# Splitting expert tails in place, another order on VectorE, and first-slot rows from one-hot products on TensorE

## The reference, cut to what matters

```
c = x @ W.T + ((x @ A[a].T) @ B[a].T) * scaling[a]     # a = adapter of the batch row
li = round(c @ w_gate.T * 128); shifted = clip(li - max(li), -128)
two largest shifted per token, ties to the lower expert; weights from an exp table, made to sum to 1
out = sum over experts e of weight_e * ((silu(c @ w1[e].T) * (c @ w3[e].T)) @ w2[e].T)
result = x + out                                        # hidden width 704 = 5 * 128 + 64
```

## Time and profile before

| | us |
|---|---|
| median of 3 runs (lowest, highest) | 231.97 (231.13, 232.19) |
| the profiled execution's own time | 231.47 |
| its span, from first to last instruction | 229.4 |
| PE busy | 205.3 |
| POOL busy | 150.7 |
| DVE busy | 100.7 |
| ACT busy | 85.5 |

### The profile page before, as it was taken

How to read it: one execution, slowest core, us unless ns; L and a number is a source line. 1 busy time by engine, 2 the same in 40 slices (tenths; PEclk the granted TensorE clock), 3 DMA queues, 4 the chain that set the end, 5 groups by cost and what they waited for, 6 DMA issues and landing times.

```text
span 229.4 us, 3961 instructions
## 1 busy us (share of the span) xinstructions
PE 205.3 (89%) x1227; PEld 176.8 (77%) x1227; DVE 100.7 (44%) x297; ACT 85.5 (37%) x232; POOL 150.7 (66%) x131
## 2 busy tenths in 40 slices
PE   7699995999999999999993799099999999999993
PEld 5479973888888888888982688088887988888891
DVE  0758886353343534344332135013533444336814
ACT  2656760599423333232331123012322323226610
POOL 8100066969969998998999799989984453188000
PEclk9999998899999999999999799859999999999999
DMA  6994317999345104064505540440051111019004
GB/s 158 414 372 160 123 60 223 379 372 331 118 161 176 37 24 139 24 206 130 171 18 188 181 139 16 169 140 23 1 186 69 70 49 69 23 47 322 22 3 183
DMA packets 16146, 32.66 MB, mean 142 GB/s; under 512 B 2080, under 2 KB 10400, under 8 KB 16000
## 3 DMA queue, kind: packets, MB, share of 16 engines
q1 hardware_dynamic: 12304, 25.17, 33.0%
q0 software_dynamic: 2160, 5.64, 7.0%
q10 hardware_dynamic: 1664, 1.61, 2.2%
HBM read 25.59 MB, written 6.82 MB: 141 GB/s over the span
## 4 chain that ended last, share of the span: by engine, by line
POOL 37%; PE 32%; DMA 14%; issue 10%; ACT 3%; POOLq 1%; DVE 1%; SPq 0%; DVEq 0%; ACTq 0%
POOL w_all L423 18%; PE gu L1095 9%; DMA rows<-cond_rows,src_i 8%; POOL rows L417 7%; POOL w_all L490 6%; PE gu L1102 4%; DMA expert_rows<-rows,dst_i 3%; DMA x<-x_t 3%; PE gu L981 3%; PE ya L1132 2%; POOL w_all L436 2%; POOL expert_rows L448 2%; PE ht L1109 2%; PE ya L1133 2%; PE ya L1134 2%
## 5 line engine op out<-in xcount | busy, mean ns | idle before, releaser
L1095 PE MATMUL gu<-w_all,xs_hi 128*128 (+2 forms) x276 | 75.2, 396 | 13.5 <-POOL w_all L436 11.8
L1095 PEld LDWEIGHTS gu<-w_all,xs_hi 128*128 128x128 f32 x276 | 48.6, 195 | 22.2 <-issue 17.5
L835 DVE TENSOR_TENSOR hid<-gu,sg 128x256 f32<-128x256 f32 x46 | 19.5, 425 | 91.9 <-ACT sg L593 88.8
L593 ACT ACTIVATE sg<-gu 128x256 f32<-128x256 f32 x46 | 17.7, 385 | 93.9 <-PE gu L1102 91.8
L423 POOL TENSOR_TENSOR w_all<-raw,w_all 128x1024 fp32r<-128x1024 f32 (+2 forms) x15 | 46.8, 3123 | 1.1
L1102 PE MATMUL gu<-w_all,xs_lo 128*128 (+1 forms) x138 | 42.1, 387 | 2.6 <-DVE xs_lo L827 2.6
L417 POOL DMA_INDIRECT rows<-cond_rows,src_i x23 | 23.1, 1005 | 30.0 <-DMA cond_rows<-c_rows 23.7
L1132 PE MATMUL ya<-w_all,h_hi 128*128 (+1 forms) x115 | 38.7, 337 | 0.0
L448 POOL DMA_INDIRECT expert_rows<-rows,dst_i x20 | 19.7, 987 | 21.1 <-DVE hid L835 8.7
L1133 PE MATMUL ya<-w_all,h_hi 128*128 (+1 forms) x115 | 32.9, 286 | 0.0
L1134 PE MATMUL ya<-w_all,h_lo 128*128 (+1 forms) x115 | 32.5, 282 | 0.0
(11 more groups left out here) (193 smaller groups left out, 280.1 us busy)
## 6 DMA issues: line engine op xcount, KB each, us to landing
raw<-expert_weights SPq DMA_DIRECT2D x6, 896.0 KB, 4.8
raw<-expert_weights SPq DMA_DIRECT2D x6, 640.0 KB
raw<-expert_weights SPq DMA_DIRECT2D x6, 512.0 KB
expert_rows<-zeros SPq DMA_DIRECT2D x1, 2048.0 KB
rows<-expert_rows SPq DMA_DIRECT2D x8, 256.0 KB, 4.7
cond_rows<-c_rows ACTq DMA_DIRECT2D x4, 256.0 KB, 2.1
raw<-x_t SPq DMA_DIRECT2D x1, 1024.0 KB
out_t<-raw SPq DMA_DIRECT2D x4, 256.0 KB, 2.2
```

What stands on the lines that cost most here:

```text
L1095: nc.tensor.matmul(out, stay_hi[:, kc * P:(kc + 1) * P], moving(at, part + first + kc * P, n), start=kc == 0 and part == HI_COLS, stop=False)
```

## The change

Five things, in the order of the kernel:

1. Expert 0's first piece is split early: ACT's cast follows `xa_hi[0]`, and DVE does the subtraction in two halves (`first_lo`) between its router operations. ACT's other casts are put in another order (`expert_hi(1, 0)` ahead of `c_copy(2)`).
2. The rows of slot 0 are not gathered. DVE makes `picks` (128 x 1024, one-hot of the position in expert 0), and PE multiplies `c_rows` with it: 16 float32 products of 128 columns, straight into the bank `xt`. They stand between the product for `src_i` and those for the destinations. The 16 products on zeros (`KEEP_WARM`) are gone. Half of `conditioned(1)` runs behind the rank count.
3. On DVE `slot_lo(0)` goes ahead of `destinations()`; `weights_of_choices` goes out of slot 0 into steps 54 to 57, its store on ACT from step 12 to step 58, and the three share gathers on POOL from ahead of scatter 7 to behind scatter 15.
4. The tail's high part is cast in place, together with the third piece (`HI_PIECES`, 1536 columns), and its low half subtracted in place. `tail_low` waits for no gather or scatter; POOL does not wait for its own `w_ready` but for expert 1; SP waits for `w_ready` instead of `raw_free[2]`. For experts 4 to 7 POOL casts piece k+1 before it subtracts piece k. One scatter goes from behind expert 5 to within expert 7.
5. PE's wait for the next slot's expert stands in the slot's last step, ahead of `down(i - 2)`, not behind it.

```diff
-GATHERED = [(0, 4), (4, 6), (6, 10), (10, 14), (14, 18), (18, 21), (21, SLOTS), (SLOTS, SLOTS)]
-SCATTERED = {4: (0, 2), 5: (2, 5), 6: (5, 6), 7: (6, 7)}
+GATHERED = [(1, 4), (4, 6), (6, 10), (10, 14), (14, 18), (18, 21), (21, SLOTS), (SLOTS, SLOTS)]
+SCATTERED = {4: (0, 2), 5: (2, 4), 6: (4, 5), 7: (5, 7)}
+SHARES_AT = ITEMS - 15
+SHARES_BEHIND = 15
+HI_PIECES = [PIECES[0], PIECES[1], slice(DOWN_AT, HI_COLS)]
...
             def tail_low(e):
-                recent = gathered_beside(e - 1, 2) if e > 1 else range(*GATHERED[0])
-                for s in [*recent, *gathered_beside(e, 0), *gathered_beside(e, 1)]:
-                    pool.wait_ge(rows_in[s], 16)
-                if e in SCATTERED:
-                    pool.wait_ge(scattered, 16 * (SCATTERED[e][0] + min(2, SCATTERED[e][1] - SCATTERED[e][0])))
-                return nc.gpsimd.tensor_tensor(stack_part(e, 1), raw_tail(e, LOWER), as_f32(tail_hi[e % 2][LOWER, :]), ALU.subtract)
+                stack = stack_part(e, LOW_HALF)
+                return nc.gpsimd.tensor_tensor(stack, raw_tail(e, LOW_HALF), as_f32(stack), ALU.subtract)
...
+                high(0)
+                for k in range(len(PIECES)):
+                    if k < 2:
+                        high(k + 1)
                     steps += 1
...
                     ins = low(e, k)
...
-                nc.gpsimd.tensor_copy(tail_hi[e % 2][:, :], raw_tail(e)).then_inc(whi_step, 1)
-                nc.gpsimd.tensor_copy(stack_part(e, 0), raw_tail(e, slice(0, TAIL))).then_inc(whi_step, 1)
-                pool.wait_ge(whi_step, steps)
                 tail_low(e).then_inc(w_ready, 1)
-                pool.wait_ge(w_ready, e + 1)
-                pool.sem_inc(raw_free[2], 1)
                 beside_piece(e, 2)
...
+                if s == SHARES_BEHIND:
+                    pool.wait_ge(share_at_ready, 1)
+                    pool.wait_ge(share_out, 16)
+                    for l in range(DIRECT):
+                        nc.gpsimd.indirect_dma_start(
...
 # DVE
             mask_part(1)
+            first_lo(0)
             xa_lo_part(1)
             pk_lo_part(slice(PK_W, PK_G), 2)
+            first_lo(1).then_inc(raw_free[0], 1)
...
+            nc.vector.tensor_tensor(picks, row_no[:, :].unsqueeze(1).broadcast_to([P, TILES, P]),
+                                    first_pos[:, :].unsqueeze(2).broadcast_to([P, TILES, P]),
+                                    ALU.is_equal).then_inc(picks_ready, 1)
...
-            for k in range(2):
-                expert_lo(0, k).then_inc(w_split0, 1)
...
+            expert_lo(1).then_inc(raw_free[1], 1)
+            slot_lo(0)
             destinations()
-            weights_of_choices()
-            expert_lo(0, 2)
-            expert_tail_lo(0)
-            slot_lo(0)
+            expert_lo(2)
+            expert_tail_lo().then_inc(w_ready, 1)
...
 # PE
+            pe.wait_ge(picks_ready, 1)
+            for kc in range(KC):
+                for t in range(TILES):
+                    pe.wait_ge(c_out, t // 2 + 1)
+                    last = nc.tensor.matmul(xt[:, kc * P:(kc + 1) * P], c_rows[:, t, kc * P:(kc + 1) * P],
+                                            picks[:, t, :], start=t == 0, stop=t == TILES - 1)
+            last.then_inc(xt_done, 1)
...
-            for _ in range(KEEP_WARM):
-                nc.tensor.matmul(gu[GU_BANKS - 1][:, :], zeros[:, :], wide_zeros, start=True, stop=True)
...
                 if 1 <= i <= ITEMS:
                     turn_hidden(i - 1)
+                if j == 2 and s + 1 < SLOTS:
+                    pe.wait_ge(w_ready, at_of[s + 1][0])
```

More of the change, by code:

```diff
@@ L129, in moe_kernel @@
         base_of = sb("base_of", [P, EXPERTS])
+        first_pos = sb("first_pos", [P, TILES])
         ends = sb("ends", [P, EXPERTS])
@@ L166, in moe_kernel @@
         h_lo = [sb(f"h_lo{i}", [P, 2 * P], F32R) for i in range(HBUFS)]
-        tail_hi = [sb(f"tail_hi{i}", [P, DIM], F32R) for i in range(2)]
+        raw_low_tail = sb("raw_low_tail", [P, DIM])
         raw = sb("raw", [P, HI_COLS])
@@ L259, in moe_kernel @@
         raw_low_in = [sem(f"raw_low_in{k}") for k in range(len(PIECES))]
-        raw_free = [sem(f"raw_free{k}") for k in range(len(PIECES))]
-        w_split0 = sem("w_split0")
+        raw_free = [sem(f"raw_free{k}") for k in range(len(PIECES) - 1)]
         w_ready = sem("w_ready")
@@ L367, in _ @@
                 raw_weights(e)
-            for k in range(len(PIECES)):
-                sp.wait_ge(raw_free[k], EXPERTS - 2)
+            sp.wait_ge(w_ready, EXPERTS)
             sp.dma_start(x_back, x_dram[:, :, :]).then_inc(x_back_in, 16)
@@ L507, in _ @@
                            allow_small_or_imprecise_dtypes=True).then_inc(pool_step, 1)
-            pool.wait_ge(share_at_ready, 1)
-            pool.wait_ge(share_out, 16)
-            for l in range(DIRECT):
-                nc.gpsimd.indirect_dma_start(
-                    out=share[:, l:l + 1], out_offset=None, in_=share_dram[:, :],
-                    in_offset=bass.IndirectOffsetOnAxis(ap=share_at[:, 2, l:l + 1], axis=0)).then_inc(share_in, 16)
             for s in range(SCATTERED[EXPERTS - 1][1], SENT):
@@ L579, in _ @@
             expert_hi(0, 2)
-            expert_tail_hi(0)
+            expert_hi(1, 0)
             c_copy(2)
             c_copy(3)
-            for k in range(len(PIECES)):
-                expert_hi(1, k)
-            expert_tail_hi(1)
+            expert_hi(1, 1)
+            expert_hi(1, 2)
             def silu(i):
@@ L760, in _ @@
                                           base_of[:, :].unsqueeze(1).broadcast_to([P, TILES, EXPERTS]), ALU.add))
+            beside(nc.vector.scalar_tensor_tensor(first_pos[:, :], by_tile(full(other))[:, :, 0], 1.0,
+                                                  picked[:, 0:TILES, 0], ALU.add, ALU.mult))
             chain(nc.vector.tensor_tensor(masked[:, :, :], mask[:, :, :],
@@ L1169, in _ @@
                 if i < ITEMS:
-                    code, at = at_of[s]
-                    if j == 0 and s:
-                        pe.wait_ge(w_ready, code)
-                    if i == 0:
-                        pe.wait_ge(w_split0, 1)
-                    if i == 1:
-                        pe.wait_ge(w_split0, 2)
-                    gate_up(i, at)
+                    if i < 2:
+                        pe.wait_ge(raw_free[i], 1)
+                    gate_up(i, at_of[s][1])
                 if j == 1 and s + 1 < SLOTS:
```

159 lines of the change are left out of this document (81 added, 78 removed).

## The result

The changed kernel takes 218.72 us (median of 4 runs, 218.49 to 218.91), the kernel before beside it 231.69 us (4 runs, 231.13 to 232.19): a ratio of 0.944, with an interval of 0.941 to 0.947. Run again later in another group of runs (e16), it took 218.45 us, ratio 0.9435 (0.941 to 0.946). What failed is the size: the start, POOL's waits and casts and the slot changes gained more than I had, and the cost at the program's end rests on a wait that neither trace has.

A forecast was written before the change was run, and what follows sets the result against it. POOL's program was taken to bound the kernel until expert 7 is ready, then PE and its feeders. POOL -9.7, `down` +0.7, slot changes -0.7 and tail +1.0 gave -8.7 us, hence 223.2 us predicted, range 220.2 to 227.2.

The forecast's parts named there:

- Start: POOL's start on expert 1, after DVE's last instruction of expert 0, comes 0.5 us sooner (range -2.4 to +3.9).
- F: Time of PE's 16 float32 products for slot 0, taken as 3.8 us (1.9 to 8.3).
- rival A: The float32 products on PE are slow, 7.6 us, so POOL starts 3.8 us later: 227.0 us; chance 14%.
- Waits for gathers: On POOL, `tail_low` of experts 1 and 2 no longer waits for rows brought by DMA: -3.2 us.
- own waits: POOL's waits for its own semaphore and the signal to SP behind experts' tails go: -2.7 us.
- casts: POOL's merged tail cast and casting the next piece early save 0.8 us for each of four experts: -3.3 us.
- `down` behind the last stall: On PE the last wait now stands ahead of `down(46)`, whose six products then delay slot 16: +0.7 us.
- Slot changes: On PE, six changes behind slot 16 lose half of a 0.22 us gap by the moved wait: -0.7 us (0 to -1.3).
- Tail: At the program's end late shares delay last scatter, read-back and first scaling by 3.2 us, PE by +1.0 (0 to +3.2).
- Rival B: The program's end keeps all of the 3.2 us delay, by ACT's in-order program: 225.4 us; chance 10%.
- rival C: PE's clock binds, falling at each of three stalls and staying low into slot 16: 225.5 us; chance 12%.
- forecast of the stalls themselves: PE's remaining stalls: 2 to 3 us at slot 12, some 4 at slot 14, 0 to 3 at slot 16.

The follow-up runs named there:

- e16: The changed kernel run once more without an edit, in another group of runs: 218.45 us, ratio 0.9435.
- e5: Changed kernel with POOL's casts of experts 4 to 7 in their old order (cast, wait, subtract; two casts for the tail): 225.61 us, ratio 0.975.
- e15: e13 with PE's wait for the next expert put back behind the down products: 220.53 us, ratio 0.953.
- e13: Changed kernel with weights of choices in steps 49 to 52 and share gathers one by one behind scatters 13, 15 and 17: 218.87 us, ratio 0.947.
- e7: Changed kernel with weights of choices in steps 56 to 59 and their store two steps later: 222.81 us, ratio 0.964.
- e6: Changed kernel with weights of choices in steps 24 to 27, store from step 28, share gathers ahead of scatter 7: 219.44 us, ratio 0.948.
- e12: Changed kernel with DVE subtracting the 1792 columns of experts 2 and 3, weights of choices in steps 49 to 52, shares behind scatter 13: 217.54 us, ratio 0.933.
- e3: Changed kernel with POOL's waits put back (gathers and scatters ahead of `tail_low`, its own `w_ready`): 227.64 us, ratio 0.981.
- e4: Changed kernel with slot 0's rows gathered and turned on PE as before, without `picks` and the 16 one-hot products: 223.92 us, ratio 0.967.
- e8: Changed kernel with DVE, not POOL, subtracting the first two pieces of experts 2 and 3: 214.12 us, ratio 0.924.
- e9: Changed kernel with PE's wait back behind the down products, weights of choices in steps 49 to 52, share gathers behind scatter 13: 221.69 us, ratio 0.955.
- e1: Changed kernel with PE's wait for the next slot's expert put back behind the slot's last down products: 222.62 us, ratio 0.959.
- e2: The kernel before with only PE's wait moved ahead of the slot's last down: 231.44 us, ratio 0.996.
- e10: Changed kernel with weights of choices in steps 49 to 52 and the share gathers behind scatter 13: 220.95 us, ratio 0.951.

## Why the prediction was wrong in size

By its own steps:

- **Start, forecast -0.5: measured -1.2.** F was right, 3.84 for 3.8, and `picks` 1.22 for 1.2, so rival A is refuted: a float32 product costs 0.24 us and a transpose 0.12, a factor of 2, both at a granted clock of 1.00. That F came out is in part luck: I took it from a 512-column product, while the trace has two records of 0.12 us for each product. The rule of the Trainium skill that I weighed ("TensorE: Matmul & The Clock Gate", section "Terms", 4 times) does not show in the trace as a price at 128 columns. Of the missing 0.7, 0.24 is the input x, whose last part landed sooner in that execution (its cast at 8.98 for 9.22); the rest is spread.
- **Waits for gathers -3.2, own waits -2.7, casts -3.3, in all -9.2: measured -10.4.** This term was mis-sized. Experts 1 to 3 gave 4.3 where I had 3.9, experts 4 to 7 6.1 where I had 5.3. e5 puts the casts at 4.3 and not 3.3 (one of its waits is mine, some 0.1). What I took from 4 rows of small gaps was a floor.
- **`down` behind the last stall +0.7: measured +0.6.** Right.
- **Slot changes -0.7 (0 to -1.3): measured -2.05.** This step failed beyond its own bound. I read the gap of 0.34 in the earlier trace rows, subtracted the usual 0.12, and gave half of the rest to the wait. e15 against e13: the whole excess of the gap goes, and the products behind it are closer too, 0.28 for each change or 1.7 in six. The other 0.4 of the 2.05 is not isolated; one slot of before has ACT idle for 1.02 us with its work ready, which may be part of it. The bound left out that the first step's own duration in the same rows, 1.19, was part of the stop.
- **Tail +1.0 (0 to +3.2): measured -0.1.** This step failed in kind: I let the first scaling wait for the read-back, and it does not. In both traces it follows ACT's cast of step 65 without idle time (208.66 and 208.93 before, 195.84 and 196.10 after), so the data had already landed and ACT's own order sets it. There was more slack still: in e7 and e13 the scaling did wait for the read-back, 1.65 and 0.74 us, and slot 22's first step to the end took 19.7 us all the same. Two sizes were off as well. The store landed in 1.4 us where the earlier trace rows had 4.2, and the gathers began 2.2 us behind its issue; against slot 22's first step the last scatter is 1.5 us later than before, the first scaling only 0.2, where I had 3.2. My row was of a store at step 12, with the weights' loads under way. In e6 the store goes out at 105.15, again with such loads, and landed in 3.8 us; in e7, at the end, in 1.4. That fits the loads as the reason, but the step differs too.

The misses are 1.9 on POOL and its start, 0.1, 1.3 and 1.1: 4.4 us, all of one sign. Rival B had the tail on the wrong side; rival C is half there, since the clock did fall behind the 5.02 us stall, but in front of another stall that took it up. The forecast of the stalls themselves (2 to 3, some 4, 0 to 3) was close to the 2.71, 5.02 and 1.14 measured. Every term fell on the cautious side; even the bounds of my range added in full give 219.7, because POOL's waits and casts had no lower bound at all.

## What to carry to other kernels

Wait for a slot's weights one piece of work ahead of where they are used: behind the last stall it costs that piece once, and at each change it saves the stop. A wait that costs nothing today can become binding when its engine gets faster; take waits and work out together. Before giving idle time of DVE to POOL's work, lay the two timelines side by side, and keep small DVE operations on SBUF away from POOL's long ones.

## What the runs showed of the hardware

**DVE and POOL take turns** when both work on SBUF: a 0.17 us operation of DVE took 3.32 and 4.86 us (e6), a 2.02 us one 3.63 and 4.09, a POOL DMA issue 2.57 for 0.96 (e12). The first two end within 0.04 us of POOL's instruction; the others end 1.9 and 0.8 us behind the other engine's, about the time that they take alone. The Trainium skill, "SBUF — State Buffer", section "SBUF: two separate sides", says that the two share a pair of ports under an exclusive lock, which a DVE operation with two SBUF inputs takes against a POOL instruction that reads SBUF. By these rows the trace agrees. DVE's operations on PSUM kept their 0.42 us beside POOL.

**A standstill of ACT and DVE**, for which no wait of the program accounts: ACT idle for 2.5 to 4.8 us in the records, most of it with PE's products done, while DVE mostly waits for ACT (on its own for 1.3 us in e3, e4, e5 and e8). It lengthens slots 16 to 22 by 1.1 us (e9 against e15) to 4.0 us (e8 against e13). It came near the end of a train of six or seven of POOL's indirect DMAs back to back in ten of the traces (e1, e3, e4, e5, e7 to e12; ACT also 1.02 us in the kernel before and 2.65 in e2, behind their own train of five from 167 on), it moved with the train from step 62 (63 in e7) to step 57, and it was absent from the traces of the three kernels whose train was cut to three (though two of e13's six executions took 220.2 and 220.4 us, so it may strike there too). e6's train of five, at 155.6, made one step 0.4 us late. And the changed kernel has a train of seven and no standstill, twice. That it goes where the train goes is shown by e10 and e13, which differ in the train alone. What else it takes is open, and so is the mechanism. A late fetch of instructions is a rival that was not tried; packets of the trace's instruction queues fall within the standstill in e3, e5, e7 and e8 and in none of the other six, which speaks against it without ruling it out.
